# A decoder layer on one Trainium2 core: row maxima spread four units to a slot and sent in eighths of the heads

## What is computed

```python
x = layernorm(x + attention(x))        # 32 heads of width 8, relative bias, softmax
x = layernorm(x + mamba(ctx) * silu(x)) # selective scan: 256 channels, 16 states, 256 steps
x = layernorm(x + top1_expert(x))      # 4 experts, width 1024
```

## Time and profile before

| | us |
|---|---|
| median of three runs | 527.64 |
| the three runs | 522.95, 527.64, 529.11 |
| profiled execution | 522.71 |
| its span | 521.0 |

### The profile page before, as it was taken

One profiled execution on the slowest core, in us unless ns is written; L12 is line 12 of the kernel. 1 busy time (PEld: TensorE's weight loads), 2 busy tenths in 40 slices (PEclk: granted clock), 3 DMA queues, 4 the chain that ended last, 5 costly groups with the idle time before them and its releaser, 6 DMA issues.

```text
span 521.0 us, 8135 instructions
## 1 busy us (share of the span) xinstructions
PE 461.8 (89%) x2763; PEld 228.1 (44%) x2764; DVE 324.0 (62%) x617; ACT 200.2 (38%) x392; POOL 217.4 (42%) x235
## 2 busy tenths in 40 slices
PE   6899938987998989989899999886989999999992
PEld 4544203332343434444344443443435666556662
DVE  3787876899997767848776566445801344333434
ACT  2565402453565437725377567200102121112210
POOL 1001042668796769945499579100081111111001
PEclk9989858999999999979999999968799999999997
DMA  8799930217154342635416420192220000000000
GB/s 218 162 213 147 307 133 1 82 42 142 43 123 102 101 82 80 137 130 162 137 48 192 163 73 0 67 371 88 81 73 9 10 10 4 8 20 10 10 2 8
DMA packets 39367, 49.39 MB, mean 95 GB/s; under 512 B 4664, under 2 KB 32673, under 8 KB 39334
## 3 DMA queue, kind: packets, MB, share of 16 engines
q1 hardware_dynamic: 36322, 46.65, 33.7%
q0 software_dynamic: 1056, 2.10, 1.3%
q10 hardware_dynamic: 1956, 0.21, 0.3%
HBM read 40.72 MB, written 8.91 MB: 95 GB/s over the span
## 4 chain that ended last, share of the span: by engine, by line
PE 59%; DVE 9%; issue 3%; ACT 2%; POOL 2%; POOLq 0%; DVEq 0%
PE ps L1092 15%; PE ps L846 9%; PE ps L1108 7%; PE ps L922 5%; PE ps L909 4%; PE ps L879 4%; PE ps L875 4%; PE ps L903 2%; PE ps L960 2%; PE ps L1100 2%; DVE arena L1403 2%; DVE arena L1446 2%; PE ps L834 2%; PE ps L989 1%; PE ps L952 1%
## 5 line engine op out<-in xcount | busy, mean ns | idle before, releaser
L1268 ACT ACTIVATE arena<-ps 128x512 f32<-128x512 f32 x128 | 76.2, 595 | 118.0 <-PE ps L909 117.9
L1403 DVE TENSOR_REDUCE arena<-ps 128x2 f32<-128x512 f32 x128 | 86.1, 685 | 31.9 <-PE ps L879 30.2
L624 POOL TENSOR_TENSOR arena<-arena 128x512 f32<-128x512 f32 x56 | 71.1, 1269 | 56.6 <-DVE arena L1446 56.5
L618 POOL TENSOR_TENSOR arena<-arena 128x512 f32<-128x512 f32 x64 | 90.0, 1408 | 2.7 <-DVE ps L1446 2.4
L1092 PE MATMUL ps<-arena 128*128 x176 | 77.5, 593 | 0.7 <-ACT arena L1294 0.6
L1446 DVE TENSOR_TENSOR_SCAN arena<-ps,arena 128x512 f32<-128x512 f32 x56 | 68.0, 1215 | 5.9 <-ACT ps L1231 4.6
L846 PE MATMUL ps<-arena,identf 128*128 128x512 f32 x128 | 70.3, 639 | 0.0
L875 PE MATMUL ps<-arena 48*128 48x256 bf16 x256 | 51.2, 281 | 18.5 <-DVE arena L1403 16.2
L1231 ACT ACTIVATE ps<-arena 128x255 f32<-128x255 f32 x128 | 60.4, 473 | 11.4 <-DVEq L1571 10.7
L1673 DVE TENSOR_TENSOR arena<-arena,ps 128x1024 f32<-128x1024 f32 x11 | 13.4, 1222 | 66.2 <-ACT arena L1298 66.2
L879 PE MATMUL ps<-hank_hi,flip 128*128 128x512 f16 x128 | 51.4, 402 | 0.0
(11 more groups left out here) (200 smaller groups left out, 542.6 us busy)
## 6 DMA issues: line engine op xcount, KB each, us to landing
arena<-bc_d SPq DMA_DIRECT2D x32, 512.0 KB, 4.1
arena<-in_L_ffn_Wg SPq DMA_DIRECT2D x8, 512.0 KB, 5.8
...
```

The lines of the kernel that those rows point to most:

```text
L618: g.tensor_tensor(dBu[m % 3], dtu[:, :, b * SEQ:(b + 1) * SEQ], over_k(bcr[c % BC_RING][:, m % 2, 0, :]), ALU.mult).then_inc(dbu_ready, 1)
L624: g.tensor_tensor(h, h, over_k(bcr[m // 2 % BC_RING][:, m % 2, 1, :]), ALU.mult).then_inc(hc_ready, 1)
L1268: A(prob[2 * (slot % 2) + kt][:, pr * HALF:(pr + 1) * HALF], ps[:, 2 + n % 2, :], ACT.Exp).then_inc(p_ready, 1)
L1403: v.tensor_reduce(negm[b % 2][:, qt, 2 * pair:2 * pair + 2], ps[:, bank, :].rearrange("p (h k) -> p h k", h=2), axis=AX.X, op=ALU.max).the ...
```

## The change

- A unit runs half a batch ahead of its scores: slots 4 to 7 of batch b hold the units of heads 0 to 15 of batch b + 1, slots 0 to 3 of batch b those of heads 16 to 31 of b itself. Each slot has four, one to a step, to (3,3). Batch 0 has 16 units in the prologue and 16 in its own slots. The halves keep one order.
- Maxima are turned, negated and sent for eight heads at a time: 16 times instead of 8. (0,0) and (0,1) in the prologue; in the loop at step 1 of every even slot, two slots ahead of the scores, except (0,0) and (3,6). `send_max` stands ahead of `load_bc` on SyncE.
- `all_taken()` goes. Tails wait for the tail step before, `route` for its own operand.
- `on_vector` holds for the second half of the last batch alone, so bank 1 is shared until (3,3), and GpSimd multiplies four more states by C.

```diff
-        negmT = [carve(SEQ // 2, dt=BF16, rows=HEADS // 2) for _ in range(2)]
+        negmT = [carve(SEQ // 2, dt=BF16, rows=8) for _ in range(2)]
...
-        A_UNITS = {slot: [] for slot in [(0, -2), (0, -1)] + [(b, qd) for b in range(BATCH) for qd in range(QUADS)]}
+        A_UNITS = {(0, -1): [(0, n // 2, n % 2) for n in range(16)]}
         for b in range(BATCH):
...
+            for qd in range(QUADS):
+                ahead = b + qd // 4
+                A_UNITS[b, qd] = [(ahead, 8 * (1 - qd // 4) + 2 * (qd % 4) + n // 2, n % 2)
+                                  for n in range(4) if ahead < BATCH]
+
+        N_EIGHTS = HEADS // 8
+
+        def eight_at(b, qd):
+
+            if qd % 2 or (b, qd) == (0, 0):
+                return None
+            ahead, e = [(b, 1), (b, 2), (b, 3), (b + 1, 0)][qd // 2]
+            return None if ahead == BATCH or (ahead, e) == (0, 1) else (ahead, e)
 
         H_BANK = 1
 
         def on_vector(m):
 
-            return m >= STATES * (BATCH - 1) and m % 2 == 1
+            return m >= STATES * (BATCH - 1) + STATES // 2 and m % 2 == 1
...
+            def send_max(b, e):
+
+                sp.wait_ge(m_ready[e], b + 1)
+                row, h = 64 * (e // 2) + ROWS, 8 * (e % 2)
+                sp.dma_start(qst[b % 2][row:row + 1, h:h + 8, :], negmT[e % 2]).then_inc(m_in[e], 16)
...
+                if eight_at(b, qd):
+                    send_max(*eight_at(b, qd))
                 if slot + BC_RING < QUADS * BATCH:
                     load_bc(slot + BC_RING)
...
-            def turn_max(b, hh):
-                pe.wait_ge(taken, max_at[b, hh])
+            def turn_max(b, e):
+                pe.wait_ge(taken, max_at[b, e])
                 bank = turn()
                 for qt in range(KT):
...
+                    last = nc.tensor.transpose(ps[0:8, bank, qt * P:(qt + 1) * P],
+                                               negm[b % 2][:, qt, 8 * e:8 * e + 8], identf[:, :])
                 last.then_inc(turned, 1)
...
                 if k < 2:
                     pe.wait_ge(pv_out, QUADS * (b + 1) + 1)
                 else:
-                    all_taken()
+                    pe.wait_ge(taken, tail_at[b, step - 1])
                 bank = turn()
+                tail_at[b, step] = turns.count
...
             def route(b):
 
-                all_taken()
+                pe.wait_ge(taken, x2_at[b])
...
-            for n, unit in enumerate(A_UNITS[0, -2]):
+            for n, unit in enumerate(A_UNITS[0, -1]):
                 scores_a(*unit)
                 if n in late_fills:
                     project, which = late_fills[n]
                     project(*which)
-            turn_max(0, 0)
+                if n == 9:
+                    turn_max(0, 0)
+            turn_max(0, 1)
             pe.wait_ge(stack_in[0][1], 16 * 2)
-            for unit in A_UNITS[0, -1]:
-                scores_a(*unit)
...
-                    if (b, qd) == (BATCH - 1, 0):
+                    if (b, qd) == (BATCH - 1, 4):
                         turns.banks = (0,)
...
-                        if (b, qd, i) == (0, 2, 3):
-                            turn_max(0, 1)
-                        if b + 1 < BATCH and (qd, i) in ((5, 1), (7, 1)):
-                            turn_max(b + 1, half_of(b + 1, qd // 7))
+                        if i == 1 and eight_at(b, qd):
+                            turn_max(*eight_at(b, qd))
```

More of the change, by code:

```diff
@@ L507, in _ @@
                 load_bc(c)
-            send_max(0, 0)
+            for e in range(2):
+                send_max(0, e)
             store_bc(1)
@@ L863, in turn @@
                 return bank
-            def all_taken():
-                pe.wait_ge(taken, turns.count)
             def begin_a(b, pair, qt):
                 bank = turn()
-                max_at[b, pair // 8] = turns.count
+                max_at[b, pair // 4] = turns.count
                 return bank
@@ L976, in turn_x2 @@
                 bank = turn()
+                x2_at[b] = turns.count
                 for i in range(4):
@@ L1557, in _ @@
                      [lambda step=step: softplus(0, step) for step in range(len(LOG1P) + 1)]
-            for n, unit in enumerate(A_UNITS[0, -2]):
+            for n, unit in enumerate(A_UNITS[0, -1]):
                 maxima(*unit)
+                if n == 9:
+                    put_max(0, 0)
                 if n % 2:
                     chores.pop(0)()
-            put_max(0, 0)
+            put_max(0, 1)
             while chores:
@@ L1571, in _ @@
             dve.sem_inc(scan_in, 1)
-            for unit in A_UNITS[0, -1]:
-                maxima(*unit)
             for b in range(BATCH):
                 for qd in range(QUADS):
-                    if (b, qd) == (BATCH - 1, 0):
+                    if (b, qd) == (BATCH - 1, 4):
                         turns.banks = (0,)
```

71 lines of the change are left out of this document (23 added, 48 removed).

## The result

| | before | after |
|---|---|---|
| median, us | 525.3 (4 runs, 517.07 to 529.11) | 499.69 (4 runs, 497.41 to 503.87) |
| ratio, 95% interval | 1 | 0.9601 (0.9537 to 0.9665) |
| profiled execution, its span | 522.71, 521.0 | 503.87, 501.9 |

What follows compares the result with a forecast made beforehand. Limits differed by stretch: VectorE, TensorE, or GpSimd level with TensorE; six units and keep_warm delayed the loop. Terms -13.4 + 0 - 2.5 + 0 - 3.0 + 5.6 - 0.5 = -13.8 gave 508.9 profiled, 511.4 median; range 503 to 522 us.

Steps and rivals of the forecast that it cites:

- Start of the loop: (0,0) and (0,1): six units and keep_warm leave the path, VectorE's prologue ends 0.9 later; -13.4 us, bounds -14.5 to -5.
- (0,2) to (0,7): Batch 0 slots: same units and softplus, VectorE still sets the time; 0 us, bounds -1 and +2.
- (1,0) to (1,4): Batch 1: stalls -2.7, two fewer lone units -1.3, three turned maxima +1.5; -2.5 us, bounds -4 and +0.5.
- (1,5) to (2,0), and (2,5) to (2,7): GpSimd's stretches: same GpSimd work, moved forward but not shortened; 0 us each, bounds -1 and +1 for the first.
- (2,1) to (2,4): Batch 2: as in batch 1 but with two turned maxima; -3.0 us, possible clock fall in (2,2) left out.
- (3,0) to (3,4): Last batch: 16 units come in, turned maxima add 1.1; +5.6 us, bounds +3 (shared bank removes waits) and +11.
- Rival C (GpSimd): Batch 3: GpSimd decides, its four more multiplications add 5.1 us in (3,0) to (3,3), none hidden; 516.5 us, chance 0.14.
- Behind the loop: After the loop: the last tail's steps stop waiting for each other's banks; -0.5 us, bounds -1 and 0.
- A: Loop's start: clock comes back late, TensorE at 1.2 GHz through (0,2), adding 8.4 us; 519.8 us, chance 0.14.
- B: Batch 0: half clock stays as slots wait for softplus, +6 us a slot; 540 us with four slots, chance 0.03.
- E: Loop: turn_max waits for a bank behind VectorE in each of 14 slots; 524.6 us, no change, chance 0.05.
- D: Batch 3's bank 1 pays for its maxima and the (2,2) disturbance, some 4.5 us, does not come; 504 us, chance 0.14.

Runs made afterwards that it cites:

- experiment 2: Kernel after with all_taken() put back in tails and route: 510.54 us, ratio 0.9817 to the kernel before.
- experiment 3: Kernel after with all_taken() put back only for the last batch's tail, behind the loop: 501.68 us, ratio 0.9664 to the kernel before.
- Experiment 5: Kernel after without keep_warm(9) ahead of the loop: 498.52 us, ratio 0.9591 to the kernel before.
- experiment 9: Kernel after without the 16 units of slots (3,0) to (3,3): 492.69 us, ratio 0.9515 to the kernel before.
- experiment 10: Kernel after with the old last batch: odd states on VectorE and bank 1 taken from the units, both from (3,0) on: 517.39 us, ratio 0.990.
- experiment 12: Kernel after with VectorE's softplus steps for batches 2 and 3 spread wider, into (1,0) and (1,2): 499.18 us, ratio 0.9607 to the kernel before.
- experiments 1: Kernel before with only the tails' and route's own waits in place of all_taken(): 509.82 us, ratio 0.9767.
- experiment 4: Kernel before without keep_warm(9) ahead of the loop, its six units kept: 525.43 us, ratio 1.013.
- experiment 11: Kernel after with units, tails and turned maxima kept to bank 0 from (3,0) on: 512.5 us, ratio 0.9881 to the kernel before.

## Why the prediction was right, and where not

- **Start of the loop: right.** Counted from the end of VectorE's prologue (0,2) begins 14.7 us earlier, where 14.3 were worked out, and by the mechanism named: ScalarE 1.00 behind the last memset, the first scan at +1.70 (predicted +1.6), (0,1) at +6.7 (+6.9). The prologue's own end was put at +0.9; the profiled execution has +4.0, but 1.35 of that is a later first unit, and 1.6 a clock that fell 15.5 us behind the first unit instead of some 18.5. From the first unit to that end it takes 30.01 before and 30.98 to 31.00 in experiments 2, 3, 5, 9 and 10, which is close to the +0.9. By the times named as signs the profiled execution misses: the first exp came at 77.53 (74 to 76 was named) and (0,2) at 89.57 (86 to 89). Experiment 5 has 74.94 and 86.05.
- **(0,2) to (0,7): 0 was 1 too low.** 48.8 in most runs against 47.64, within the bounds of -1 to +2. Whether the units' new places or the clock make the 1.1 stays open: every profile of the kernel after and its variants (but experiment 12's, which has other work there) has some 3.4 us or more at half clock in this stretch, and those of the kernel before and of experiments 1 and 4, which have 47.62 to 47.64, have none.
- **(1,0) to (1,4): right in the sum, and each part too small.** Stalls 3.15 instead of 2.7, two units 1.70 instead of 1.3, and turned maxima 0.55 in (1,0), 0.81 in (1,2), 0.83 in (1,4), so 2.2 instead of 1.5. That -2.6 met -2.5 is luck: what was missed on either side cancels.
- **(1,5) to (2,0), and (2,5) to (2,7):** -0.5 and -0.8 against 0. Both keep their 28.09 and 20.82 in experiment 1, so they don't come from the tails' waits; no run separates them further.
- **(2,1) to (2,4): -3.0 against -5.2**, of which 1.3 is clock: (2,2) lost 2.9 us to it before (14.40, against 11.50 in experiment 4) and 1.6 after (11.71, against 10.07). Without the clock it is -3.9; the stall in (2,2) is 2.2 us and not the 1.12 (twice 0.56) taken over from (1,2).
- **(3,0) to (3,4): right in the sum**, +5.2 against +5.6, and the units are its cause, as stated, but its parts were off: 4.5 for 16 units and 1.1 for the turned maxima. The 16 units with all that waits for them are 5.5 (0.34 each), and without them the slots take no more than before. Rival C (GpSimd) falls with experiment 9. The bound of +3 counted on waits that the shared bank removes; with one bank for the units the slots are 12 us longer (experiment 11).
- **Behind the loop: this step was wrong.** The term said that the last tail's steps "no longer wait for each other's banks: -0.5, bounds -1 and 0". It measured -4.0 from put_y to the second addition, outside its bounds: 2.2 for the exchanges, 1.9 for a fallen clock beneath them. The mechanism was the one named, and its size was wrong. Another 2.0 us between there and the logits are the route's own wait and the clock, which the runs don't separate: of these 2.0 experiments 2 and 4 have 1.1 (a clock of 0.77 and 0.85 in the next 17 us), and experiment 3, whose route does not wait, 1.0. The prediction had priced the same wait at 0.56 and 0.78 in the loop and did not carry that price to the four waits behind the loop, where it would have given 2.2.
- **(3,5) to the end of the loop, and the rest**: -1.5 and +1.5 are clock. (3,5) to the end takes 18.07 and 18.08 in experiments 1 and 4, which change nothing there, and 19.62 before, with 3.4 us at half clock from 324 on. The rest takes 157.8 in the kernel after and in experiment 9, which both have 3.4 us at half clock some 19 us behind the logits, and 156.0 to 156.3 in all the others.
- **Rivals.** A: the clock did start the loop at half (0.62 over the first two slots) and was back in (0,1), so the 8.4 us that it priced did not come. Up to 1.4 us of it is measured, in (0,1); in (0,0) its price is open. B and E fall (B's time for four slots is 543.8 by its own terms, not 540). Seven turned maxima waited for a unit's maximum, 4.5 us in all, which the list of waits shows; one of the seven, 0.79, stands in the prologue:

```profile
PE ps L923 <- DVE arena L1397: 4.5, 7, 1.6
```

  D's time, 504, is the nearest to the measured one, but only a part of its reason holds: the disturbance in (2,2) was 1.3 us smaller, and the larger surplus came from behind the loop.
- **The rule on the clock.** By "TensorE: Matmul & The Clock Gate" of the Trainium skill, section on HAM oscillation, keep_warm buys nothing in its new place, since TensorE waits behind it. Experiment 5 agrees (11.11 without; 12.04, 11.06 and 11.11 with). The prediction took the 0.54 ahead of the loop as a sign of the rule; the record of the clock puts that fall at 61.1, ahead of the 8.56 us of idling (65.0 to 73.56), when TensorE had been busy 7.07 of the last 7.10 us. So the idling did not bring that fall about.

What stays open: what decides whether the clock falls in the prologue, in (2,2), near (3,2) or behind the loop in a given execution. Experiment 4 has all the stalls of the kernel before and kept 1.00 in (2,2).
